# A macaron block with a gated delta rule: betas from eight products, w1 loaded beside the recurrence, and a recurrence loop with its outputs one to two chunks behind

## What is computed

```python
x = x + 0.5 * ffn(layernorm(x))            # 512 -> 64 units, each a small relu net of 16 -> 512
x = x + attn(layernorm(x))                 # below
x = x + 0.5 * ffn(layernorm(x))

def attn(x):
    h = rmsnorm(x, ln1)
    q, k, v = h @ wq + bq, h @ wk + bk, h @ wv + bv      # 16 heads of 32
    k = k / (norm(k) + 1e-6)
    beta = sigmoid(h @ wbeta + bbeta)                    # one for each head and token
    for t in range(8192):                                # for each head, S is 32 x 32
        S = S + beta_t * outer(v_t - S @ k_t, k_t)
        o_t = S @ q_t
    x = o @ wo + bo + x
    return gelu(rmsnorm(x, ln2) @ w1 + b1) @ w2 + b2 + x  # 512 -> 2048 -> 512
```

## Time and profile before

| | |
|---|---|
| median of three executions | 3515.68 us (3514.63 to 3520.36) |
| the profiled execution: time, span | 3515.62 us, 3513.6 us |
| TensorE busy with products, with weight loads | 3297.1 us (94%), 2607.9 us (74%) |
| DVE, ScalarE (ACT), POOL busy | 1833.6, 1322.4, 1154.8 us |
| granted TensorE clock, mean | 0.974 |
| stage 1, stage 2, stage 3 from about | 0, 1008, 1823 us |

### The profile page before, as it was taken

How to read it: one execution, slowest core, us unless ns; L and a number is a source line. 1 busy time by engine, 2 the same in 40 slices (tenths; PEclk the granted TensorE clock), 3 DMA queues, 4 the chain that set the end, 5 groups by cost and what they waited for, 6 DMA issues and landing times. The chain is left out here.

```text
span 3513.6 us, 150217 instructions
## 1 busy us (share of the span) xinstructions
PE 3297.1 (94%) x68430; PEld 2607.9 (74%) x68430; DVE 1833.6 (52%) x2940; ACT 1322.4 (38%) x2630; POOL 1154.8 (33%) x1223
## 2 busy tenths in 40 slices
PE   3999999999959999999978999999999999999997
PEld 2777777777747888888866777777777777777775
DVE  4777777777649777787313332332333233333332
ACT  3544444444313333333333333333333333333332
POOL 0336464646427555555201220212222111122220
PEclk7999999999979999999988999999999999999998
DMA  3344555554466666665552011011100101111010
GB/s 95 109 145 152 155 152 152 152 156 150 131 192 189 194 194 191 195 199 177 171 157 90 13 36 37 24 36 36 37 29 20 36 25 36 37 36 37 13 36 24
DMA packets 388097, 355.41 MB, mean 101 GB/s; under 512 B 58128, under 2 KB 320912, under 8 KB 384912
## 3 DMA queue, kind: packets, MB, share of 16 engines
q1 hardware_dynamic: 385632, 351.27, 32.0%
q10 hardware_dynamic: 2224, 0.90, 0.1%
HBM read 184.19 MB, written 153.09 MB: 96 GB/s over the span
## 5 line engine op out<-in xcount | busy, mean ns | idle before, releaser
L1782 DVE TENSOR_TENSOR glo<-gl,gh 128x512 fp32r<-128x512 f32 x256 | 195.1, 762 | 926.0 <-ACT gh L1689 925.8
L1685 ACT ACTIVATE gl<-bank,b1m 128x512 f32<-128x512 f32 x256 | 175.9, 687 | 796.5 <-PE bank L235 796.5
L233 PE MATMUL bank<-w_hi,gh 128*128 128x512 f32 x1024 | 410.8, 401 | 24.9 <-DVE glo L1782 24.9
L233 PE MATMUL bank<-h_hi,w_hi 128*128 128x512 f32 x1024 | 425.8, 416 | 4.0 <-DVE w_lo L1826 4.0
L235 PE MATMUL bank<-w_hi,glo 128*128 128x512 f32 x1024 | 406.9, 397 | 0.0
L235 PE MATMUL bank<-h_hi,w_lo 128*128 128x512 f32 x1024 | 406.7, 397 | 0.0
L234 PE MATMUL bank<-h_lo,w_hi 128*128 128x512 f32 x1024 | 406.5, 397 | 0.0
L234 PE MATMUL bank<-w_lo,gh 128*128 128x512 f32 x1024 | 405.6, 396 | 0.0
L233 PEld LDWEIGHTS bank<-w_hi,gh 128*128 128x128 f32 x1024 | 193.1, 189 | 75.8 <-DVE glo L1782 31.9
L1187 PE MATMUL bank<-ringA 32*32 32x32 f32 x16512 | 238.7, 196 | 7.7 <-issue 6.1
L233 PEld LDWEIGHTS bank<-h_hi,w_hi 128*128 128x128 f32 x1024 | 193.1, 189 | 58.5 <-issue 10.7
(11 more groups left out here) (170 smaller groups left out, 7071.4 us busy)
## 6 DMA issues: line engine op xcount, KB each, us to landing
ringB<-heads_scratch SPq DMA_DIRECT2D x256, 192.0 KB, 2.7
ringA<-heads_scratch SPq DMA_DIRECT2D x258, 128.0 KB, 2.2
X<-in_L_attn_x SPq DMA_DIRECT2D x16, 1024.0 KB, 9.7
x_scratch<-X SPq DMA_DIRECT2D x16, 1024.0 KB, 4.7
heads_scratch<-vb SPq DMA_DIRECT2D x16, 1024.0 KB, 5.2
heads_scratch<-qk SPq DMA_DIRECT2D x16, 1024.0 KB, 6.9
heads_scratch<-kb SPq DMA_DIRECT2D x16, 1024.0 KB, 5.2
heads_scratch<-kbuf SPq DMA_DIRECT2D x16, 1024.0 KB, 7.1
```

What stands on the lines that cost most here:

```text
L233: e.matmul(o, lhs[0], rhs[0], start=first, stop=False)
L1685: e.activation(gl[k][:, :], bank[k][:, :], ACT.Gelu_apprx_tanh, bias=b1m[:, m:m + 1]).then_inc(a_gl, 1)
L1782: e.tensor_tensor(gh[k][1][:, :], gl[k][:, :], gh[k][0][:, :], ALU.subtract).then_inc(v_gl, 1)
```

## The change

In words:

- Betas. One tensor `wb` takes the place of the high and low part of wbeta: its columns 32h to 32h + 3 hold the high part and columns 32h + 16 to 32h + 19 the low part. `project` for the betas makes two products in each of four pieces, wb by the high and wb by the low part of h, eight in all. The eviction only adds the bias (from `bbeta`, zero in the new columns). After the transpose, DVE adds the two parts (128x64) and ScalarE's new `gate(t)`, after evict(t, 1), applies the sigmoid to 128x64 and writes `bg1`. POOL's `betas` goes.
- w1. The high and low parts of w1 live through stages 2 and 3. In stage 2, from turn 6 on and in every second turn, one of 16 pieces is split (ScalarE at chunk 1 of the turn, DVE at chunk 2) from two buffers of their own; SP issues its load two turns earlier. Stage 3 loads only the 16 pieces of w2. Three are split ahead of the first tile; the others one by one after the gelus of the first tile. The waits of `up` for w1 go.
- The loop of stage 2. TensorE's turn is laid out anew. sT has four buffers in place of two. The outputs of chunk 3 are made in the next turn, those of chunks 0, 1 and 2 one or two half steps later than before. The twelve wo products are two groups of six, at j = 2 and 3, in place of three groups of four. `high` and `low` of both pairs move to chunks 0 and 1 of the next turn, `add_out` to chunk 0 of the turn after that. SP's order of loads and their waits follow. Ahead of the loop TensorE also waits for ringA slots 2 and 3 and ringB slots 0 and 3.

The core of the diff:

```diff
@@ project
-                    m = product(e, bank[bk][:, :], (w[0][:, f, c], w[1][:, f, c]),
-                                (hT1[0][:, f, :], hT1[1][:, f, :]), f == 0, f == NF - 1)
+                    if kind == "b":
+                        e.matmul(bank[bk][:, :], wb[:, f, :], hT1[0][:, f, :], start=f == 0, stop=False)
+                        m = e.matmul(bank[bk][:, :], wb[:, f, :], hT1[1][:, f, :], start=False, stop=f == NF - 1)
...
@@ act_project
+            def gate(t):
+                e.wait_ge(v_bsum, t + 1)
+                if t >= 2:
+                    e.wait_ge(o_kb, 4 * (t - 1))
+                e.activation(bg1[t % 2][:, :, :], bs[:, :, 0:GROUPS], ACT.Sigmoid).then_inc(a_bg, 1)
...
@@ turn_beta
                 e.transpose(flat(bs[:, :, :]), proj[(13 * t) % 2][:, :]).then_inc(v_bs, 1)
+                e.wait_ge(v_bs, t + 1)
+                e.tensor_tensor(bs[:, :, 0:GROUPS], bs[:, :, 0:GROUPS], bs[:, :, 16:16 + GROUPS],
+                                ALU.add).then_inc(v_bsum, 1)
...
@@ sp_delta
             for blk in range(NBLK + 1):
                 c = 4 * blk
-                if c + 6 < CHUNKS + 2:
+                if c + 6 < CHUNKS + 4:
                     load_a(c + 6)
-                if c + 4 < CHUNKS:
+                if blk and c + 3 < CHUNKS:
+                    load_b(c + 3)
+                if c + 7 < CHUNKS + 4:
+                    load_a(c + 7)
+                if c + 4 <= CHUNKS:
                     load_b(c + 4)
-                if c + 7 < CHUNKS + 2:
-                    load_a(c + 7)
                 if c % NC == 12 and c // NC + 2 < NS:
                     load_system(c // NC + 2)
+                i = piece2(blk + 2)
+                if i is not None:
+                    if i >= 2:
+                        e.wait_ge(v_w1lo, i - 1)
+                    e.dma_start(w1s[i % 2][:, :], pieces2[i][0]).then_inc(d_w1s[i % 2], 16)
...
@@ pe_delta, the turn after the change (old: delta, out_state, ahead(2) or keys/values; state, out_delta, ...)
                         delta(j)
                         if j == 0:
+                            ahead(2)
+                        elif j == 1:
+                            ahead(3)
+                        elif j == 2:
+                            out_state(1)
+                            out_delta(1)
+                            e.wait_ge(d_A[0], next_a)
+                            e.reg_add(next_a, next_a, 32)
+                            keys(0)
+                        else:
+                            out_state(2)
+                            out_delta(2)
+                            keys(1)
+                        e.wait_ge(a_delta, now)
+                        if j in (1, 2):
+                            e.wait_ge(d_B[j], slot_b)
+                        e.reg_add(now, now, 1)
+                        state(j)
+                        if j == 0:
+                            out_state(3)
+                            out_delta(3)
+                        elif j == 1:
                             e.wait_ge(v_olo, out)
                             e.reg_add(out, out, 4)
+                            out_state(0)
+                            out_delta(0)
+                        elif j == 2:
+                            values(0)
+                            e.wait_ge(v_olo, out)
+                            e.wait_ge(v_z, out)
+                            e.reg_add(out, out, 4)
+                            out_product(range(0, 6))
+                            e.wait_ge(d_B[3], slot_b)
+                            e.reg_add(slot_b, slot_b, 16)
+                            e.wait_ge(d_A[1], slot_a)
+                        else:
+                            values(1)
+                            out_product(range(6, 12))
                             e.wait_ge(d_A[2], slot_a)
                             e.wait_ge(d_A[3], slot_a)
                             e.reg_add(slot_a, slot_a, 32)
...
@@ act_delta
             for c in range(CHUNKS):
                 blk, at = divmod(c, 4)
-                if at == 3:
-                    high(2 * blk)
                 delta(c)
                 if c + 1 < CHUNKS:
                     keys(c + 1)
-                if at == 0 and blk:
-                    high(2 * blk - 1)
                 state(c)
+                if at < 2 and blk:
+                    high(2 * blk - 2 + at)
...
                 if at == 0 and blk:
                     normalize(blk - 1)
+                i = piece2(blk)
+                if at == 1 and i is not None:
+                    e.wait_ge(d_w1s[i % 2], 16 * (i // 2 + 1))
+                    e.activation(pieces2[i][1], w1s[i % 2][:, :], ACT.Copy).then_inc(a_w1hi, 1)
...
@@ dve_delta
-                if at == 0 and blk:
-                    low(2 * blk - 1)
-                if at == 3:
-                    low(2 * blk)
-                    if blk:
-                        add_out(blk - 1)
+                if at == 0 and blk >= 2:
+                    add_out(blk - 2)
                 solver(c, 0)
+                if at < 2 and blk:
+                    low(2 * blk - 2 + at)
+                i = piece2(blk)
+                if at == 2 and i is not None:
+                    e.wait_ge(a_w1hi, i + 1)
+                    e.tensor_tensor(pieces2[i][2], w1s[i % 2][:, :], pieces2[i][1], ALU.subtract).then_inc(v_w1lo, 1)
                 solver(c, 1)
...
@@ act_dense, and the same in dve_dense
-            for i in range(NP3):
+            for i in range(AHEAD3):
                 split(i)
             for t in range(NT):
                 for m in range(NM):
                     gelu(t, m)
+                    if t == 0 and m + AHEAD3 < NP3:
+                        split(m + AHEAD3)
```

More of the change, by code:

```diff
@@ L377, in project @@
                 bk, c = (13 * t + j) % 3, slice(g4 * P, (g4 + 1) * P)
-                w = wp[kind]
                 if t == 0 and kind == "b":
@@ L386, in project @@
                         bank_free(bk)
-                    m = product(e, bank[bk][:, :], (w[0][:, f, c], w[1][:, f, c]),
-                                (hT1[0][:, f, :], hT1[1][:, f, :]), f == 0, f == NF - 1)
+                    if kind == "b":
+                        e.matmul(bank[bk][:, :], wb[:, f, :], hT1[0][:, f, :], start=f == 0, stop=False)
+                        m = e.matmul(bank[bk][:, :], wb[:, f, :], hT1[1][:, f, :], start=False, stop=f == NF - 1)
+                    else:
+                        w = wp[kind]
+                        m = product(e, bank[bk][:, :], (w[0][:, f, c], w[1][:, f, c]),
+                                    (hT1[0][:, f, :], hT1[1][:, f, :]), f == 0, f == NF - 1)
                 m.then_inc(p_proj, 1)
@@ L517, in evict @@
                         proj_free(t, j)
-                    e.activation(proj[slot][:, :], bank[bk][:, :], ACT.Sigmoid,
+                    e.activation(proj[slot][:, :], bank[bk][:, :], ACT.Identity,
                                  bias=bbeta[:, 0:1]).then_inc(a_ev, 1)
@@ L608, in act_project @@
                 evict(t, 1)
+                gate(t)
                 if nxt:
@@ L1012, in pool_project @@
             for t in range(NT):
-                betas(t)
                 if t:
@@ L1036, in pool_project @@
             beta_k(NT - 1, 3)
+        w1 = sbuf(top, "w1_hi", [P, NF, DFF], F32R), sbuf(top, "w1_lo", [P, NF, DFF], F32R)
+        pieces2 = []
+        for n in range(4):
+            c = slice(n * D, (n + 1) * D)
+            pieces2 += [(a["L0_attn_w1"][k * P:(k + 1) * P, c], w1[0][:, k, c], w1[1][:, k, c]) for k in range(NF)]
+        LOAD2, NP2 = 4, len(pieces2)
         with ExitStack() as st:
+            w1s = [sbuf(st, f"w1s{i}", [P, D]) for i in range(2)]
             wo = sbuf(st, "wo_hi", [P, NF, D], F32R), sbuf(st, "wo_lo", [P, NF, D], F32R)
@@ L1072, in macaron, with piece2 @@
         d_x1b, d_z = sems("d_xb0 d_xb1"), sems("d_z0 d_z1")
+        d_w1s, (a_w1hi, v_w1lo) = sems("d_w1s0 d_w1s1"), sems("a_w1hi v_w1lo")
+        def piece2(blk):
+            i, r = divmod(blk - LOAD2 - 2, 2)
+            return i if r == 0 and 0 <= i < NP2 else None
         p_R, p_delta, p_state, p_o, p_wo = sems("p_R p_delta p_state p_o p_wo")
@@ L1099, in load_a @@
                 s = chunk // NC
-                if c > 4 and c % 4 == 0:
-                    e.wait_ge(p_o, c - 4)
+                if c >= 4 and c % 4 < 2:
+                    e.wait_ge(p_delta, max(1, c - 4))
                 elif c >= 4:
@@ L1214, in delta @@
             def delta(j):
-                tiles(place(j), nR[j % 2], sT[j % 2], False).then_inc(p_delta, 1)
+                tiles(place(j), nR[j % 2], sT[j], False).then_inc(p_delta, 1)
             def out_state(j):
-                tiles(outputs(j), sT[j % 2], split(ringB[:, j, RQ, :]), j % 2 == 0)
+                tiles(outputs(j), sT[j], split(ringB[:, j, RQ, :]), j % 2 == 0)
             def state(j):
```

115 lines of the change are left out of this document (43 added, 72 removed).

## The result

The changed kernel takes 3432.13 us (median of 4 runs, 3426.17 to 3435.07), the one before 3515.15 (4 runs, 3512.27 to 3520.36). The ratio is 0.976, with a 95% interval of 0.9742 to 0.9778: 83 us less, of which the forecast had 61.6. The profiled execution took 3430.42 us, its span is 3428.6.

What follows compares the result with a forecast made beforehand. TensorE was taken to bound the kernel, with the turn's length deciding stage 2. Betas -15.0, stage 2 -24.9 and stage 3 -21.7 summed to -61.6, from the median 3515.68 to 3454 us, range 3428 to 3479.

Steps and rivals of the forecast that it cites:

- disturbances in them: Stage 2 loop: late ringB in five turns after a 2 MB system load; 9.3 us falls to 2.7, gaining 6.6.
- start of the loop: Ahead of stage 2's loop: four more load waits and two more memsets add 1 us (0 to 4.2).
- stage 3: Start of stage 3: pauses of 3.97 and 16.21 and slow products of 2.09 go, z's load adds 0.6: -21.7 us.
- the rival that set the low end: Stage 2 loop: turn goes to 11.2 us, edge hidden under wide products, four-set steps 1.15: 3430 us, chance 0.15.
- The turn: Stage 2 loop: eight half steps sum to 11.62 us against 12.02, 0.40 less, 22.8 us over 57 turns.
- The last half step: state(3) in the loop: values, six wo products and a back edge of 0.26, partly covered: 2.55 us.
- The four-set half step with waits: delta(2) in the loop: 1.38 us, as the old first half step with four sets and two groups of waits.
- The four-set half step without waits: delta(3) in the loop: four sets, no wait within, between 1.00 and 1.38, taken as 1.20 us.
- d1: Loop, delta of chunk 1 up to its state: ScalarE's high ahead of the normalization adds 0.20, giving 1.20 us.
- s2: Loop, state of chunk 2 up to the next delta: values and six wo products, 2.29 us.
- One wide group fewer: Loop: the saving is mostly one change of form fewer; by the tiling-mode rule alone, 0.32 us a group.
- The turn's bounds: Loop: 11.1 us without ScalarE delay, edge hidden, cheap fourth sets; 12.3 with 0.39 delay, 0.30 more edge, four-set steps 1.5.

Runs made afterwards that it cites:

- edge_small: Kernel after with one set of small products (values(1)) moved behind the turn's last six wide wo products, so the back edge follows small products: 3452.87 us.
- three_groups: Kernel after with its twelve wo products in three groups of four instead of two of six: 3439.3 us.
- best: Kernel after with late ScalarE normalization, system loads in quarters, and stage 1's two first-system transposes behind g sums, X additions and their statistics: 3412.61 us.
- w1_only: Kernel before with only the w1 part of the change, its pieces at the same places of the old turn: 3491.63 us.
- ahead16: Kernel after with all 16 splits of w2 made ahead of the first gelu instead of three: 3443.39 us.
- betas_only: Kernel before with only the betas part of the change: 3499.25 us.
- unrolled: The kernel best with TensorE's loop of 64 turns written as 32 turns of two blocks: 4320.53 us.

## Why the prediction was right, and where it was off

Term by term, forecast and trace:

```
up to the first betas product      0       +0.3
betas                            -15.0    -15.8
turns, 8 to the last             -22.8    -44.2   (median 11.98 to 11.19, 56 turns)
disturbances in them              -6.6     -3.3   (excess over 56 plain turns 11.5 to 8.2)
                 + late oT_lo     +1.5     in the line above
last turn, up to its last state  in turns  -1.4
first seven turns                  0       -1.9
start of the loop                 +1.0     +2.7
end of the loop                   +2.0     +1.7
stage 3                          -21.7    -23.0
sum                              -61.6    -85.1   (spans 3513.6 to 3428.6)
```

The right column goes by the two profiled executions, and so adds up to the difference of their spans (-85.1 before the rows are rounded); the medians differ by 83. The forecast had the direction and two of three terms. That 3432 lies inside its range is owed to the rival that set the low end, not to its own sum.

- **Betas:** 64 products at 0.234, about all of it on the path. Shown in the whole (15.8) and alone (14.4).
- **The turn** is the term that failed, and by its size, not its kind: -0.79 a turn, not -0.40. Four entries were too long. The last half step, six products and 0.26 for the edge: 2.55 against 2.38, and the 0.12 that it has over s2 does not even stand at the edge. The four-set half step with waits, taken from the first of the old order: 1.38 against 1.25. The four-set half step without waits, between bounds of 1.00 and 1.38: 1.20 against 1.15. d1, by a delay on ScalarE: 1.20 against 1.15. Together 0.17 + 0.13 + 0.05 + 0.05, with 0.03 in s2, 0.43 in all. The forecast named this very case as a rival, turn 11.2, edge hidden and four-set steps at 1.15, 3430, and gave it 0.15. It is what happened.
- What misled: the old first half step (1.38) has four sets too, but it stands right behind the edge and holds four waits. d3 of the kernel after, four sets with neither, takes 1.15, and d2, four sets with one wait, 1.25; so the 0.38 was not the price of a fourth set. How much of it was the edge's and how much the waits', no run tells. In edge_small the half step behind the edge has three sets and no waits, and takes 0.99. The earlier trace rows had the better price beside it, 0.28 a set where nothing is waited for.
- **One wide group fewer** was named as the chief gain. A group costs 0.29 in its half step, and one more costs 0.18 of the turn net (three_groups). The edge is the larger part of the 0.79, 0.44 by edge_small, and the forecast gave it 0.04 (0.30 to 0.26). The 0.17 that is left no run isolates.
- The turn's bounds, 11.1 and 12.3, don't follow from the terms named for them: those give 10.8 (four sets at 4 x 0.28) and 12.5. The 2.7 that stays of the ringB waits should be 5 x 0.5 = 2.5. The range and the chances didn't hang on either.
- **ringB:** 8.7 to 4.6, not to 2.7. The load in quarters takes the rest away (no ringB entry in best).
- **DVE** doesn't bound the turn, as forecast. From turn 8 on the late oT_lo cost 2.0 in 6 waits where 1.5 was allowed. In the first seven turns these waits grew from 3.8 to 6.9 us, and the seven became 1.9 shorter all the same.
- **w1 pieces:** turns with one are no longer than turns without, in the kernel after (median 11.19 against 11.18) and in w1_only (12.00 against 12.00). Counting nothing was right.
- **Stage 3:** the late load_z(1) shows where it was forecast, at m = 13 of the first tile, as a wait of 0.37 for glo instead of 0.6; in ahead16 it is gone. Of the 1.3 by which 23.0 exceeds 21.7, 1.0 lies between the first up-product and the first down-product. The two `up` there took 8.0 us behind the old pause of 3.97 and take 7.0 now, at a mean granted clock of 0.69 (1843 to 1851) and 0.79 (1777 to 1784.3). The forecast had priced the slow products behind the second pause only.
- **Start of the loop:** four waits more for loads and two memsets, +2.7 for the +1 counted, within its bound of 4.2. betas_only and w1_only, with the old loop, have 6.5 and 8.8 us there for the 7.8 of the kernel before, so 1 us of it can be scatter.

## What to carry over

In a loop where the engine issues without a break, put the wide instructions last: their execution covers the edge, which was worth 0.44 us a turn here, more than the wide group saved. Don't take a half step that stands behind a loop's edge and holds waits as the price of one that has neither; a set beside it with neither was the better price. Where a wait for a slower engine's queue is removed, look at what is next in that queue (g, then X, then rawk here), and move the filler behind all of it.

## What the runs showed of the chip that I had not expected

- The edge of a TensorE loop of 64 turns costs some 0.56 us behind a set of small products, and nothing that the trace shows behind six or four products of 128x512 (edge_small, the kernel after, three_groups).
- A group of wide products among 32x32 ones costs 0.29 to 0.33 us beside its products, into the form and back; one more costs the turn 0.18 net, as a break of 0.12 elsewhere goes with it (three_groups).
- The body of this loop, 24 sets of 32 products and 12 wide ones with their weight loads, runs without issue waits in its middle; with twice that a turn goes from 11.2 to 25.7 us, with 9.24 MB on the instruction queue instead of 2.52 (unrolled).
- The first turn of the loop takes 28 us (1003.4 to 1031.7 in the kernel after) against 11.2, with an issue wait of 6.8 ahead of it and others of up to 4.4 in it. In the other kernels with one turn in the body it is 26.6 to 30.8, the kernel before among them.
- 0.15 us in the third half step of every kernel here but unrolled, before and after, on TensorE itself: its cause is open.
